# Row maxima of layer 1 turned into rows, value bias folded into the output bias, and a new order of tasks

## The chip, the cores and the metric

One Trainium2 chip, the program on one of its cores. The metric is the device time of one execution in microseconds; of the kernel before, three runs were taken, and the median is the figure that counts.

## The reference, cut to what is computed

The input x is 16 batches of 256 rows by 512, the context 16 x 256 x 384. Four sublayers follow one another, each added to x:

- Layer 0 cross-attention on LayerNorm(x): `Qp = query @ Wq + bq`, K and Q divided by their row norms, 16 heads of 32, softmax of the scaled scores, `out @ Wo + bo`, plus Qp, then LayerNorm with gamma and beta.
- Layer 0 feed-forward: LayerNorm, a Hadamard product, rounding to 4-bit levels by row, a product with ternary weights.
- Layer 1 cross-attention on LayerNorm(x): the parts that matter here are

```
v = (key_value @ Wv + bv) ...
attn = jnp.einsum('bhqd,bhkd->bhqk', q, k) * scale
attn = jnp.clip(attn, -CLAMP, CLAMP)
attn = jax.nn.softmax(attn, axis=-1)
x = jnp.einsum('bhqk,bhkd->bqhd', attn, v).reshape(B, Nq, Cq)
return x @ Wo + bo
```

- Layer 1 feed-forward: LayerNorm, ternary W1 to 2048, GELU, ternary W2 back to 512.

The rows of a softmax sum to one, so `attn @ (kW + bv) @ Wo + bo` equals `attn @ (kW) @ Wo + (bv @ Wo + bo)`.

## The kernel before, in words

**Two phases.** Phase A (about the first 1376 us) does the two attentions and the layer 0 feed-forward, batch by batch. Phase B does the layer 1 feed-forward two batches at a time, and the change doesn't touch it.

**Streams and steps.** A batch passes four streams of tasks: `front_0` (part 0f: norm, turns, projections of q, k and v), `heads_of(0) + back(0)` (0b: scores, exp, attend, output product, feed-forward 0), `front_1` (1f) and `heads_of(1) + back(1)` (1b). In step i, stream n works on batch i-n, so four batches are in work at once. There are 19 steps, 0 to 18. In steps 3 to 15 all four streams are active and the string ORDER merges their task lists: each digit names the stream that gives the next task. ORDERS has an own string for steps 0, 1, 2, 16, 17 and 18, where `PREPARE` adds a fifth stream (weights to split, signs to take). Every engine walks through the same merged list and issues its part of each task, so ORDER sets the order of work on each engine's queue; semaphores make an engine wait where a task's input is not there. The eight PSUM banks are handed out along the same order by `banks_of`.

**Numbers.** Products are made of fp16 halves: `product` (L1285 on) does three matmuls of 512 columns per chunk (L1289, L1290, L1293), and with a bias a fourth one, L1292, of a bias row pair held as [128, 512] and a column that chooses the pair's two rows. `project` tasks with j = 2 are the values; with j = 0 and 1 they are q and k of layer 0. `project_turned` (L1299 to L1303) makes q and k of layer 1 turned, 13 + 13 matmuls of 256 columns for j = 0 (4 chunks of three, and the bias), 10 + 10 for j = 1.

**Layer 1's softmax.** In `front_1`, `maxima` makes the 16 heads' scores with the queries as rows (four heads, a quad, at once, each on 32 rows of the array: L1430), and DVE's `reduce` (L1113) takes each row's maximum. After 8 heads DVE's `shifts` (L1118) clips them into `mcut` [128, 2, 16] fp16. One step later, in `heads_of(1)`, `scores` makes the scores of a quad again, now with the keys as rows, in four PSUM banks. DVE's `clip` (L1123) clips each bank in place. PE's `head` then waits for the clip of its own head and subtracts the maxima, which must now lie along the columns: two matmuls of 256 columns per head (L1445), whose stationary side is the column `mcut[:, q, n]` broadcast to 128 and whose moving side is minus the identity. It then attends head n-4: 12 matmuls of 33 or 32 columns (L1463 to L1465). ScalarE's `head` takes exp (L905) and the upper fp16 half (L913), GpSimd's the lower half (L759). After each quad DVE's `attn_out` divides (L1203, L1206).

**The rest that is named later.** `clip` is the DVE's work at L1123; `out` of layer 0 is L1142 plus statistics (L1031, L1033); `post_norm` is L1152, L1154 and statistics; `split_qk` of layer 1 is L1106; `turn_ffn`, `turn_x`, `turn_out` are four fp32 transposes (L1309); `hadamard` is eight matmuls (L1381). GpSimd computes the reciprocal deviations between DVE's statistics and the next use (L726 to L732). The store of x1 (L774) comes once a step, from GpSimd's queue.

**Setup.** All engines but SP begin by waiting until GpSimd has made CONSTS = 18 constants (L701 to L720). SP loads the first context and x at once, then, after the constants, twelve bias rows (L603). `split_bias` turns them into three fp16 pairs on ScalarE and DVE.

Three places of the code carry this, the merge, the wait per head and the order in the queue:

```
def merged(streams, order):
    streams = [list(x) for x in streams]
    out = [streams[int(n)].pop(0) for n in order]
...
                    pe.wait_ge(clipped.sem, clipped.at(b, n + 1))
...
                        mm = te.matmul(out[:, :, q, :], mcut[:, q, n:n + 1].to_broadcast([P, P]),
                                       minus.unsqueeze(1).to_broadcast([P, NT, P]), start=False, stop=True,
```

Of the kernel before, what the change touches and what calls it, by code (L numbers as in the profile page):

```python
# [63 lines left out]
class Chain:  # L64
# [5 lines left out]
    def __call__(self, ins):  # L70
# [7 lines left out]
ORDER = ("0021312111112210000002010100001110011011100131330003333101033333031133113113102113331133312322102323"  # L78
         "13032123232321321313113031113033131012230120123303230222023222223232121320222020010121220011212")
ORDERS = {  # L80
    0: ("000400000000000440000000000000404000000000000000"),
    1: ("0111111110111040001001101001001011010101010000110111010111011404141414441000100100110000111001011111"
         "01111111404"),
    2: ("2011111121101210011001210012101112000010100101020001011011101012102211020121211200220020000221221111"
         "222220222212220121102012012121021212112101221"),
    B: ("1311333133113113211131112121311211321233413133323333231333321312111214333314313113133411222233121213"
         "3131431222214113123231221322323132221232442222242212121121211"),
    B + 1: ("2334332333333343323322343324333333323423233223343443333224344232233334442222233232322222224223222222"
         "2243223223"),
    B + 2: ("33333333334333433334343333333343333333333343334343344343443444434333"),  # L90
# [10 lines left out]
def fills(task):  # L101
# [4 lines left out]
             "tern_sum": "tw", "tern_turn": "tt", "mean_sum": "ms", "turn_signs": "sg"}  # L106
# [14 lines left out]
def frees(task):  # L121
# [4 lines left out]
              "tern_sum": "tw", "tern_turn": "tt", "mean_sum": "ms", "turn_signs": "sg"}  # L126
# [58 lines left out]
def front_1():  # L185
# [30 lines left out]
def back(l):  # L216
# [13 lines left out]
    0: [("weight", 0), ("weight", 1), ("bias_split", 0), ("weight", 2), ("weight", 3)],  # L230
    1: [("tern_signs", 0), ("tern_sum", 0)] + [("tern_turn", c) for c in range(DC)] + [("weight", n) for n in range(4, 8)],
# [7 lines left out]
APART = [FRONT_TURNS[0] + FRONT_TURNS[1], BACK_TURNS[0] + BACK_TURNS[2], BACK_TURNS[1] + BACK_TURNS[2]]  # L239
STREAMS = [front_0(), heads_of(0) + back(0), front_1(), heads_of(1) + back(1)]  # L240
# [15 lines left out]
def kept_apart(tasks):  # L256
# [3 lines left out]
    late = ("normalise", 1) in at and ("round", 0, 0) in at and at["normalise", 1] > at["round", 0, 0]  # L260
    return all(b < c or d < a for a, b, c, d in pairs) and not late
# [32 lines left out]
def steps(emit):  # L294

    base, kept = [[0] * 8] * 2, {}
    for i in range(B + len(ALL) - 1):
        tasks = task_order(i)
        uses, counts = plan([task for _, task in tasks], base)
        kept.update({name: use for name, use in uses.items() if name[0] in ("tw", "tt", "sg")})  # L300
        emit(tasks, i, i % 2, {**kept, **uses})
        base = plus(base, counts)
# [3 lines left out]
def xattn_ffn(nc, t):  # L306
    with ExitStack() as ctx:
# [25 lines left out]
        half_ones = take(1).bitcast(F16)  # L333
        row_names = ["L0_xattn_bq", "L0_xattn_bk", "L0_xattn_ln_gamma", "L0_xattn_ln_beta"]
        rows = {n: take(D) for n in row_names}
        bias_names = ["L0_xattn_bv", "L0_xattn_bo", "L1_xattn_bq", "L1_xattn_bk", "L1_xattn_bv", "L1_xattn_bo"]
        bias_pairs = [take(D // 2).bitcast(F16) for _ in range(len(bias_names) // 2)]
        bias_rows = {n: (bias_pairs[k // 2], half_ones[:, k % 2:k % 2 + 1]) for k, n in enumerate(bias_names)}
# [69 lines left out]
        mcut = tiny(NT * H // 2).bitcast(F16).rearrange("p (t h) -> p t h", t=NT)  # L408
# [5 lines left out]
        one_col = tiny(1)  # L414

# [28 lines left out]
        CONSTS = 18  # L444
# [1113 lines left out]
```

## Time and profile before

| | |
|---|---|
| median of three runs | 1841.64 us (1840.3 to 1843.56) |
| profiled execution, first to last instruction | 1838.4 us |
| PE busy | 1722.9 us, 94%, 18714 matmuls |
| DVE busy | 1209.7 us, 66% |
| ScalarE busy | 1067.7 us, 58% |
| GpSimd busy | 925.6 us, 50% |
| mean granted TensorE clock | 0.978 |
| L1445, the shift | 512 matmuls |
| L1292, bias of values and of the output product | 128 matmuls |

The profiled execution has no separate device time on record; its span is 3.2 us under the median of the runs, and the median contains what lies around the span. In the rows below matmuls overlap (starts lie closer together than one lasts), so what a matmul costs its successors is read from the distance between starts. "L1123 ... x4" is four instructions in a row, with the time from the first's start to the last's end. A bracket at the end of a row is idle time of the engine before it and what ended it.

### The profile page before, as it was taken

The page shows a single profiled execution, that of the slowest core. Times are in us where ns is not written, and L with a number is a line of the kernel's source. Part 1 is how long each engine was busy: PE and PEld are TensorE (multiplying, and loading weights), DVE is VectorE, ACT ScalarE, POOL GpSimd, SP SyncE. Part 2 cuts the span into 40 slices and gives each one's busy share as a digit, 9 for nine tenths or more (in the row PEclk, how much of TensorE's full clock was granted, in tenths as well). Part 3 has the DMA queues.
Part 4 walks back from the last instruction along what each step waited for, and adds up shares of the span by engine and source line. Part 5 has one row for each costly group of instructions (what it writes and reads, how often), then busy time and mean ns, then how long its engine had stood idle before and what let it go on. Part 6 is the DMA issues. An engine that isn't in the chain of part 4 may idle for free. (4 is left out here: it accounts for less than half of the span.)

```text
span 1838.4 us, 45922 instructions
## 1 busy us (share of the span) xinstructions
PE 1722.9 (94%) x18714; PEld 1052.9 (57%) x18714; DVE 1209.7 (66%) x2446; ACT 1067.7 (58%) x1970; POOL 925.6 (50%) x1062
## 2 busy tenths in 40 slices
PE   5789999999999999999999999979769999999999
PEld 2455666666666666666666666655544444444443
DVE  5658778687786867768687786849973433344332
ACT  5675866868677586876868667576552222222221
POOL 1663846748466484755848467464462222222221
PEclk9789999999999999999999999989979999999999
DMA  7122020211202112020220202045320111011100
GB/s 234 44 86 80 6 96 2 96 51 47 96 2 97 42 56 96 3 96 21 77 92 6 96 2 97 17 158 189 106 97 0 47 47 46 1 46 47 46 24 23
DMA packets 46343, 115.56 MB, mean 63 GB/s; under 512 B 5420, under 2 KB 9644, under 8 KB 45112
## 3 DMA queue, kind: packets, MB, share of 16 engines
q1 hardware_dynamic: 43832, 104.25, 16.4%
q0 software_dynamic: 2304, 8.39, 1.1%
q8 instruction: 150, 2.46, 0.6%
q14 instruction: 57, 0.47, 0.1%
HBM read 72.78 MB, written 31.46 MB: 57 GB/s over the span
## 5 line engine op out<-in xcount | busy, mean ns | idle before, releaser
L759 POOL TENSOR_TENSOR arena<-arena 128x512 f16<-128x512 f32 x512 | 568.8, 1135 | 159.2 <-ACT arena L913 159.1
L905 ACT ACTIVATE arena<-psum 128x512 f32<-128x512 f32 x512 | 309.8, 612 | 54.4 <-PE psum L1430 31.3
L913 ACT ACTIVATE arena<-arena 128x512 f16<-128x512 f32 x512 | 329.2, 651 | 1.0 <-PE psum L1465 1.0
L963 ACT ACTIVATE arena<-psum,arena 128x512 f32<-128x512 f32 x128 | 88.3, 690 | 352.6 <-PE psum L1483 352.6
L1289 PE MATMUL psum<-arena 128*128 128x512 f16 x672 | 258.2, 384 | 7.5 <-ACT arena L905 4.0
L1290 PE MATMUL psum<-arena 128*128 128x512 f16 x672 | 255.4, 380 | 0.0
L1293 PE MATMUL psum<-arena 128*128 128x512 f16 x672 | 255.0, 379 | 0.0
L789 POOL TENSOR_TENSOR arena<-arena 128x512 f16<-128x512 f32 x64 | 73.1, 1142 | 341.4 <-DVE arena L1233 341.4
L1483 PE MATMUL psum<-arena 128*128 128x512 f16 x1024 | 243.6, 380 | 1.4 <-DVE arena L1226 1.4
L1493 PE MATMUL psum<-arena 128*128 128x512 f16 x1016 | 239.9, 378 | 1.0 <-POOL arena L789 1.0
L1233 DVE CAST arena<-arena 128x512 f16<-128x512 f32 x128 | 54.8, 428 | 271.8 <-ACT arena L963 271.8
L1463 PE MATMUL psum<-arena 128*128 128x33 f16 x2048 | 202.0, 179 | 23.1 <-POOL arena L759 21.4
L771 POOL TENSOR_TENSOR arena<-arena 128x512 f32<-128x512 f32 x32 | 41.8, 1329 | 327.3 <-DVE arena L1177 327.3
L1463 PEld LDWEIGHTS psum<-arena 128*128 128x128 f16 x2048 | 171.8, 97 | 54.6 <-issue 18.4
L1465 PE MATMUL psum<-arena 128*128 128x33 f16 x2048 | 199.4, 178 | 0.4 <-issue 0.4
L1464 PE MATMUL psum<-arena 128*128 128x32 f16 x2048 | 199.2, 177 | 0.0
L1309 PE MATMUL psum<-arena 128*128 128x128 f32 x992 | 149.9, 288 | 38.4 <-ACT arena L835 13.5
L1123 DVE TENSOR_SCALAR psum<-psum 128x512 f32<-128x512 f32 x256 | 160.7, 691 | 24.4 <-PE psum L1430 24.2
L1464 PEld LDWEIGHTS psum<-arena 128*128 128x128 f16 x2048 | 166.0, 97 | 13.8
L1042 DVE TENSOR_TENSOR arena<-psum,arena 128x512 f16<-128x512 f32 (+1 forms) x192 | 123.1, 663 | 75.2 <-ACT arena L840 73.9
L1483 PEld LDWEIGHTS psum<-arena 128*128 128x128 f16 x1024 | 99.8, 98 | 124.7 <-issue 2.7
L1430 PE MATMUL psum<-arena 32*128 32x256 f16 x4608 | 163.2, 272 | 8.5 <-DVE arena L1086 3.0
(123 smaller groups left out, 3329.5 us busy)
## 6 DMA issues: line engine op xcount, KB each, us to landing
arena<-in_x SPq DMA_DIRECT2D x32, 512.0 KB, 4.6
arena<-x_scratch SPq DMA_DIRECT2D x32, 512.0 KB, 5.7
arena<-in_L_ffn_W SPq DMA_DIRECT2D x16, 1024.0 KB, 5.2
arena<-arena SPq DMA_DIRECT2D x16, 512.0 KB, 6.5
x_scratch<-arena POOLq DMA_DIRECT2D x16, 512.0 KB, 6.2
x_scratch<-arena SPq DMA_DIRECT2D x16, 512.0 KB, 3.0
out<-arena SPq DMA_DIRECT2D x14, 512.0 KB, 3.8
arena<-in_ctx SPq DMA_DIRECT2D x16, 384.0 KB, 5.7
```

What stands on the lines that cost most here:

```text
L759: gp.tensor_tensor(pl[l][:, h % NP, :], pf[l][:, h % NF, :], ph[l][:, h % NP, :], ALU.subtract).then_inc(p_lo[l].sem, 1)
L905: sc.activation(pf[l][:, h % NF, :], bank(u.bank), ACT.Exp, scale=SCALE / (QS * QS) if l == 0 else SCALE).then_inc(read[u.bank], 1)
L913: sc.activation(ph[l][:, h % NP, :], pf[l][:, h % NF, :], ACT.Copy).then_inc(p_hi[l].sem, 1)
L1289: te.matmul(out, x_hi, w[:, 0, c, :], start=(c == 0), stop=False)
L1290: te.matmul(out, x_hi, w[:, 1, c, :], start=False, stop=False)
L1293: mm = te.matmul(out, x_lo, w[:, 0, c, :], start=False, stop=(c == chunks - 1))
L1430: mm = te.matmul(bank(u.bank)[:, k * S:(k + 1) * S], parts[own][rows_g, j, m, k * P:(k + 1) * P], parts[other][rows_g, 1 - j, m, :], start ...
L1463: te.matmul(out, p_hi_t, vs[l][:, k, h, 0:OW], start=(k == 0), stop=False)
L1464: te.matmul(out[:, 0:HD], p_hi_t, vs[l][:, k, h, HD + 2:VP], start=False, stop=False)
L1465: mm = te.matmul(out, p_lo_t, vs[l][:, k, h, 0:OW], start=False, stop=(k == NT - 1))
L1483: mm = te.matmul(bank(4 + f % 2), w1T[:, c, f * P:(f + 1) * P], xTb[slot][:, part, c, :], start=(c + part == 0), stop=(c + part == DC))
L1493: mm = te.matmul(bank(k), src[:, f % NG, k * P:(k + 1) * P], w2T[:, f, :], start=(f + n == 0), stop=(f + n == FC))
```

## The change

- **Shift by rows.** New task `turn_max` in `front_1`, after each `shifts`: PE multiplies `mcut[:, q, :]` (now [128, 2, 128] fp16, of which the columns 32g + m hold head 4m + g) with minus the identity, two matmuls of 128 columns, which gives the negated maxima as rows; ScalarE copies them as fp16 into `max_turned` [128, 256], one per 8 heads. New task `shift` in `heads_of(1)`, after the four clips of a quad: PE waits for the quad's fourth clip and does four matmuls, one per head and bank, with 32 rows and 512 columns: stationary a column that chooses one of the 32 rows, broadcast to 128, moving `max_turned` repeated twice. `head` no longer shifts.
- **Value bias folded.** The values are projected without bias. Once per layer a new task `fold` computes bv @ Wo in 12 matmuls of 512 columns and adds it to bo in the stage of bias rows; the output product still has its bias matmul, of one tile per layer. GpSimd places bv in columns (`place_bv`); SP loads bv as columns and 8 bias rows instead of 12.
- **Setup.** CONSTS goes from 18 to 21: two memsets of 128x1024 fp16 and one of 128x256 fp16 come in, one memset of 128x512 fp32 goes, and four small additions (three of them in a chain) take the place of three small memsets.
- **Order.** ORDER and all ORDERS are new, and `BEFORE` demands that the last shift of a batch comes before `shifts` and `turn_max` of the next one.

The diff, cut to its core:

```diff
+ORDER = ("2011120111212102000011010000100111013011010333301100300310123113133311302331301133222233103313330331"
+         "3311132223121333132133213331131103011303033112221233003322202203222122322323222202222202001020111201"
+         "1")
...
     for m in range(H // HG):
         out += [("maxima", 1, m)] + [("reduce", 1, h) for h in quad(m)]
         if m * HG % EARLY_MAXIMA == EARLY_MAXIMA - HG:
-            out += [("shifts", 1, m * HG // EARLY_MAXIMA)]
+            out += [("shifts", 1, m * HG // EARLY_MAXIMA), ("turn_max", 1, m * HG // EARLY_MAXIMA)]
...
-            out += [("clip", 1, h) for h in quad(m)]
+            out += [("clip", 1, h) for h in quad(m)] + [("shift", 1, m)]
...
-    0: [("weight", 0), ("weight", 1), ("bias_split", 0), ("weight", 2), ("weight", 3)],
-    1: [("tern_signs", 0), ("tern_sum", 0)] + [("tern_turn", c) for c in range(DC)] + [("weight", n) for n in range(4, 8)],
+    0: [("weight", n) for n in range(4)] + [("fold", 0)],
+    1: [("tern_signs", 0), ("tern_sum", 0)] + [("tern_turn", c) for c in range(DC)] + [("weight", n) for n in range(4, 8)] + [("fold", 1)],
...
-                        mm = product(bank(u.bank), src, wsplit[l, "qkv"[j]], k, n, 2 * late, n if late else 2,
-                                     bias_rows[f"L{l}_xattn_bv"] if j == 2 else None)
+                        mm = product(bank(u.bank), src, wsplit[l, "qkv"[j]], k, n, 2 * late, n if late else 2)
...
+                    elif kind == "turn_max":
+                        u = use["mt", 1, k]
+                        pe.wait_ge(shift_ready.sem, shift_ready.at(b, k + 1))
+                        open_bank(u)
+                        for q in range(NT):
+                            mm = te.matmul(bank(u.bank)[:, q * P:(q + 1) * P], mcut[:, q, :], minus, start=True, stop=True)
+                        mm.then_inc(filled[u.bank], 1)
+                    elif kind == "shift":
+                        if k % 2 == 0:
+                            all_read(pe, [use["mt_before", 1, k // 2]])
+                        pe.wait_ge(clipped.sem, clipped.at(b, HG * k + HG))
+                        for g, h in enumerate(quad(k)):
+                            rows_g = slice(g * HD, (g + 1) * HD)
+                            te.matmul(bank(use["s", 1, h].bank), chosen[rows_g, k:k + 1].to_broadcast([HD, P]),
+                                      max_turned[k // 2][rows_g, :].unsqueeze(1).to_broadcast([HD, NT, S]), start=False, stop=True,
+                                      skip_group_check=True).then_inc(shifted.sem, 1)
...
+                    elif kind == "fold":
+                        u = use["fd", l]
+                        pe.wait_ge(w_split, split_by(l, "o"))
+                        pe.wait_ge(bv_placed, 4 * l + 4)
+                        open_bank(u)
+                        for c in range(DC):
+                            for n, (x, w) in enumerate(((0, 0), (0, 1), (1, 0))):
+                                mm = te.matmul(bank(u.bank), bv_sel[l][:, x, c, :], wsplit[l, "o"][:, w, c, :],
+                                               start=(c + n == 0), stop=(c == DC - 1 and n == 2))
...
-            def head(l, i, b, n, use):
-                if l == 1 and n < H:
-                    if n % EARLY_MAXIMA == 0:
-                        pe.wait_ge(shift_ready.sem, shift_ready.at(b, n // EARLY_MAXIMA + 1))
-                    pe.wait_ge(clipped.sem, clipped.at(b, n + 1))
-                    u = use["s", 1, n]
-                    out = bank(u.bank).rearrange("p (k t n) -> p k t n", k=NT, t=NT)
-                    for q in range(NT):
-                        mm = te.matmul(out[:, :, q, :], mcut[:, q, n:n + 1].to_broadcast([P, P]),
-                                       minus.unsqueeze(1).to_broadcast([P, NT, P]), start=False, stop=True,
-                                       skip_group_check=True)
-                    mm.then_inc(shifted.sem, 1)
+            def head(l, b, n, use):
```

Merged with the streams, the orders give these lists of tasks in a steady step between the scores of quad 2 of layer 1 and the shift of quad 3 (a number after the kind is the layer, the next the tile, head or quad). Before:

```
scores 1 2; clip 1 8; out_project 0 0; out_project 0 1; clip 1 9; clip 1 10; clip 1 11; out 0 0; normalise 1;
head 1 8; turn_x 1 0; turn_x 1 1; out 0 1; norm 0 1; split_x 1 0; head 1 9; split_x 1 1; head 1 10;
post_norm 0 0; head 1 11; unit 0 1; scores 1 3; project_turned 1 0 0; post_norm 0 1; split_qk 1 0 0;
clip 1 12; project_turned 1 0 1; clip 1 13; split_qk 1 0 1; clip 1 14; project 1 0 2 0; normalise_ffn 0 0;
clip 1 15; project 1 0 2 1; normalise_ffn 0 1; head 1 12; turn_ffn 0 0; head 1 13; turn_ffn 0 1;
split_ffn 0 0; head 1 14; turn_qk 0 0 0; head 1 15
```

After:

```
scores 1 2; out_project 0 1; clip 1 8; clip 1 9; clip 1 10; unit 0 1; clip 1 11; shift 1 2; out 0 0;
head 1 8; head 1 9; out 0 1; post_norm 0 0; post_norm 0 1; head 1 10; project_turned 1 0 0; split_qk 1 0 0;
project_turned 1 0 1; head 1 11; normalise_ffn 0 0; split_qk 1 0 1; normalise_ffn 0 1; scores 1 3;
clip 1 12; clip 1 13; turn_ffn 0 0; clip 1 14; project 1 0 2 0; turn_ffn 0 1; clip 1 15; shift 1 3
```

Head 8 carries on DVE the division of the first quad (`attn_out`) in both.

## Rows read from the trace of the kernel before

**Rows 1.** The first line of the page.

```profile
span 1838.4 us, 45922 instructions
```

**Rows 2.** Steady stretch, busy us (instructions): PE, PEld, DVE, ACT, POOL; granted clock, DMA.

```profile
250.00:1150.00 900.00, 878.13 (x11840) 587.18 (x11839) 686.35 (x1466) 662.07 (x1281) 564.24 (x676) 1.00 0.17 58
```

**Rows 3.** GpSimd in order of time (start us, us), the store of x1.

```profile
254.48 0.61 POOL L774 DMA_DIRECT2D x_scratch<-arena  x1 [0.30 <-POOL arena L771]
...
1114.04 0.61 POOL L774 DMA_DIRECT2D x_scratch<-arena  x1 [0.30 <-POOL arena L771]
```

**Rows 4.** PE in order of time: two heads' shift, one head's attend.

```profile
741.95 0.60 PE L1445 MATMUL psum<-arena 128*128 128x256 f16 x4
742.38 0.18 PE L1463 MATMUL psum<-arena 128*128 128x33 f16 x1
...
742.69 0.38 PE L1289 MATMUL psum<-arena 128*128 128x512 f16 x1
```

**Rows 5.** PE in order of time: a bias matmul, a quad of scores.

```profile
707.70 0.38 PE L1292 MATMUL psum<-arena 128*128 128x512 f16 x1
707.92 0.38 PE L1293 MATMUL psum<-arena 128*128 128x512 f16 x1
708.23 0.83 PE L1430 MATMUL psum<-arena 32*128 32x256 f16 x24
709.00 0.39 PE L1289 MATMUL psum<-arena 128*128 128x512 f16 x1
```

**Rows 6.** All engines in order of time, setup.

```profile
4.63 1.54 PE L1309 MATMUL psum<-arena 128*128 128x128 f32 x6 [4.63 <-POOL arena L720]
...
5.43 0.70 DVE L1031 BATCH_NORM_STATS2 arena<-arena 128x6 f32<-128x512 f32 x1 [5.43 <-DMA arena<-in_x]
```

**Rows 7.** DVE in order of time, one steady step.

```profile
521.25 0.69 DVE L1142 SCALAR_TENSOR_TENSOR arena<-psum,arena 128x512 f32<-128x512 f32 x1
...
522.85 0.18 DVE L1203 RECIPROCAL arena<-psum 128x8 f32<-128x8 f32 x1
...
524.00 0.69 DVE L1142 SCALAR_TENSOR_TENSOR arena<-psum,arena 128x512 f32<-128x512 f32 x1 [0.45 <-PE psum L1293]
...
527.06 0.74 DVE L1152 SCALAR_TENSOR_TENSOR arena<-arena 128x512 f32<-128x512 f32 x1
...
529.49 1.64 DVE L1152 SCALAR_TENSOR_TENSOR arena<-arena 128x512 f32<-128x512 f32 x1
...
532.82 0.66 DVE L1106 SCALAR_TENSOR_TENSOR arena<-psum,arena 128x512 f16<-128x512 f32 x1
533.40 1.29 DVE L1123 TENSOR_SCALAR psum<-psum 128x512 f32<-128x512 f32 x2
534.59 0.68 DVE L1106 SCALAR_TENSOR_TENSOR arena<-psum,arena 128x512 f16<-128x512 f32 x1
535.19 1.29 DVE L1123 TENSOR_SCALAR psum<-psum 128x512 f32<-128x512 f32 x2
```

**Rows 8.** PE in order of time, the same step.

```profile
527.83 0.28 PE L1299 MATMUL psum<-arena 128*128 128x256 f16 x1
...
533.52 0.38 PE L1289 MATMUL psum<-arena 128*128 128x512 f16 x1
...
536.20 0.64 PE L1309 MATMUL psum<-arena 128*128 128x128 f32 x4
536.67 0.38 PE L1445 MATMUL psum<-arena 128*128 128x256 f16 x2
```

**Rows 9.** GpSimd in order of time, the same step.

```profile
528.32 2.26 POOL L759 TENSOR_TENSOR arena<-arena 128x512 f16<-128x512 f32 x2
```

**Rows 10.** PE in order of time, step 16.

```profile
1275.94 0.38 PE L1445 MATMUL psum<-arena 128*128 128x256 f16 x2 [1.28 <-DVE psum L1123]
```

**Rows 11.** PE around that wait: stretch, its length, busy us, granted clock, DMA.

```profile
1274.60:1277.80 3.20, 1.38 (x9) 1.00 1.04 397
1277.90:1281.30 3.40, 3.40 (x36) 0.50 0.34 139
```

More of the change, by code:

```diff
@@ L239 @@
 APART = [FRONT_TURNS[0] + FRONT_TURNS[1], BACK_TURNS[0] + BACK_TURNS[2], BACK_TURNS[1] + BACK_TURNS[2]]
+BEFORE = [(("normalise", 1), ("round", 0, 0)), (("shift", 1, H // HG - 1), ("shifts", 1, 0)),
+          (("shift", 1, H // HG - 1), ("turn_max", 1, 0))]
 STREAMS = [front_0(), heads_of(0) + back(0), front_1(), heads_of(1) + back(1)]
@@ L259, in kept_apart, with kept_uses @@
     pairs = [[at[task] for task in x] for x in APART if all(task in at for task in x)]
-    late = ("normalise", 1) in at and ("round", 0, 0) in at and at["normalise", 1] > at["round", 0, 0]
-    return all(b < c or d < a for a, b, c, d in pairs) and not late
+    in_order = all(at[a] < at[b] for a, b in BEFORE if a in at and b in at)
+    return all(b < c or d < a for a, b, c, d in pairs) and in_order
+def kept_uses(uses):
+    kept = {name: use for name, use in uses.items() if name[0] in ("tw", "tt", "sg")}
+    return {**kept, **{("mt_before", *name[1:]): use for name, use in uses.items() if name[0] == "mt"}}
 assert all(kept_apart([task for _, task in task_order(i)]) for i in range(B + len(ALL) - 1))
@@ L299, in steps @@
         uses, counts = plan([task for _, task in tasks], base)
-        kept.update({name: use for name, use in uses.items() if name[0] in ("tw", "tt", "sg")})
         emit(tasks, i, i % 2, {**kept, **uses})
+        kept.update(kept_uses(uses))
         base = plus(base, counts)
@@ L716, in _, with place_bv @@
                 gp.memset(vs[l][:, :, :, HD:HD + 2], 1.0).then_inc(const_ready, 1)
-            gp.memset(half_ones, 0.0).then_inc(const_ready, 1)
-            for n in range(2):
-                pool.wait_ge(const_ready, CONSTS - 2 + n)
-                gp.memset(half_ones[n * 2 * HD:(n + 1) * 2 * HD, n:n + 1], 1.0).then_inc(const_ready, 1)
-            pool.wait_ge(const_ready, CONSTS)
+            for l in range(2):
+                gp.memset(bv_sel[l], 0.0).then_inc(const_ready, 1)
+            gp.memset(mcut, 0.0).then_inc(const_ready, 1)
+            gp.tensor_tensor(row_of, identh[:, 0:4], identh[:, HD:HD + 4], ALU.add).then_inc(const_ready, 1)
+            for n in range(1, P // HD):
+                source = identh[:, 0:HG] if n == 1 else chosen
+                gp.tensor_tensor(chosen, source, identh[:, n * HD:n * HD + HG], ALU.add).then_inc(const_ready, 1)
+                pool.wait_ge(const_ready, CONSTS - (P // HD - 1) + n)
+            def place_bv(l):
+                pool.wait_ge(bv_loaded, 16 * 2)
+                hi, lo = ([bv_sel[l][:, s, :, row:row + 1] for row in (0, HD)] for s in range(2))
+                bv = bv_cols[:, l, :].unsqueeze(2)
+                for place in hi:
+                    gp.tensor_copy(place, bv).then_inc(bv_placed, 1)
+                pool.wait_ge(bv_placed, 4 * l + 2)
+                for place, upper in zip(lo, hi):
+                    gp.tensor_tensor(place, bv, upper, ALU.subtract).then_inc(bv_placed, 1)
             def rstd(name, ts):
@@ L933, in step @@
                         split_weight(l)
-                    elif kind == "bias_split":
-                        split_bias()
+                    elif kind == "fold":
+                        upper_bias(l, use["fd", l])
+                    elif kind == "turn_max":
+                        u = use["mt", 1, at[0]]
+                        act.wait_ge(filled[u.bank], u.filled_at)
+                        sc.activation(max_turned[at[0]], bank(u.bank)[:, 0:S], ACT.Copy).then_inc(read[u.bank], 1)
                     elif kind == "tern_sum":
@@ L1180, in step @@
                         split_weight(l)
-                    elif kind == "bias_split":
-                        split_bias()
+                    elif kind == "fold":
+                        fold_bias(l, use["fd", l])
                     elif kind == "tern_signs":
```

96 lines of the change are left out of this document (55 added, 41 removed).

## The prediction

> **What bounds it now.** The span is 1838.4 us [rows 1], the median of the runs 1841.64, so I add 3.2 us to any span. I read the busy times over a long stretch first, then step marks, then PE and DVE in order of time inside one step. Between 250 and 1150 us PE is busy 878 of 900 us at full clock; DVE 686, ACT 662, POOL 564 [rows 2]. The store of x1 comes once a step, at 254.48 and, 11 steps later, at 1114.04 [rows 3]: 78.1 us a step, of which PE is idle 1.9. PE is the bound, so matmul time taken out counts in full, as long as PE finds its next input ready. ORDER rules the 13 steps in which all four streams run (3 to 15).
>
> **PE time removed.** (a) The shift. Four matmuls of 256 columns (L1445) start the next work 0.43 us later [rows 4], so 0.1075 each; 32 a step are 3.44 us. The new one does four 32-row matmuls of 512 columns per quad. No row shows that form; the nearest is the quad of scores (L1430), 24 matmuls of 256 columns on 32 rows in 0.77 us, which is 0.128 per round of four, and it starts 0.09 us after the slot of the product before it ends (707.92+0.217=708.14, against 708.23) [rows 5]. Two such rounds and the gap give 0.36 a quad, 1.44 a step, which I take, since its row groups and banks are the same. Bounds: 0.22 (one 512-column slot) and 0.87 (no overlap of the four). Gain 2.0 a step, between 2.6 and 0.
> The Trainium skill, "TensorEngine Tiling (Array Packing)", Key Properties, says that a change of tiling mode drains TensorE, which speaks against a new switch per quad. By the row that drain is the 0.09 just counted; the page gives no figure.
> (b) The bias matmul of the values (L1292), 0.217 from its start to the next [rows 5], four a step: 0.87. (c) Added: four matmuls of 128 columns a step (turn_max); by half and by the whole of a 256-column slot 0.2 to 0.43, I take 0.3. Their ACT copy is one of 128x256 twice a step; ACT is idle over a quarter of the stretch [rows 2] and nobody reads the copy before the next step, so nothing; with ACT full it would be about an exp's time each.
> Net 2.57 us a step. Over the 16 batches 41 us. Against it, once: two folds of 12 matmuls (24 x 0.217 = 5.2, partly in idle time of the first steps, 0 to 5.2, I take 4) and longer setup. PE's first matmul starts when GpSimd's constants are done, 4.63; DVE's statistics wait for x until 5.43 [rows 6], so 0.8 is hidden. Three bigger memsets and a chain of four small additions replace one memset and three tiny ones: between 0 and 3 us more, I take 1.8, and 1 shows. SP has 8 small bias row loads instead of 12 plus two loads of columns, before first use in both cases: nothing. The second rounding of weights is as before. If all else stood, 1841.6-41+5 = 1805.
>
> **The wait that the new order adds.** Before, head n of layer 1 waited for its own clip; now the shift waits for the fourth clip of the quad. I expanded both orders and added rows along the two queues, between the scores of quad 2 and the use of quad 3, since DVE can't begin the clips of quad 2 before PE has made those scores.
> DVE, new order: 4 clips, out, attn_out, out, post_norm twice, split_qk twice, 4 clips. From [rows 7]: two clips take 1.19 (533.40 to 534.59), so 2.4 for four; out 1.60 (521.25 to 522.85); attn_out 0.70 (522.85 to 524.00 less the 0.45 waited); the first post_norm 2.43 (527.06 to 529.49), the second 3.33 (529.49 to 532.82); split_qk 0.58. Sum 2.4+1.6+0.7+1.6+2.43+3.33+1.16+2.4 = 15.6, with 0.1 of tail and 0.1 to start: 15.8 us after the scores' slot.
> PE, new order, from the same point to the shift of quad 3: out_project 13 x 0.217 = 2.82, shift 0.36, four heads' attend at 0.31 (742.38 to 742.69) [rows 4] = 1.24, two project_turned 5.69 (527.83 to 533.52), scores 0.86, two turn_ffn at 0.47 (536.20 to 536.67) [rows 8] = 0.94, six matmuls of the values 1.30. Sum 13.2.
> So PE waits 15.8-13.2 = 2.6 us there in each of 13 steps. In the order before, the quad's clips end at 535.19+1.29 = 536.48 [rows 7], and PE makes the second of its four shifts at 536.67 [rows 8], with a feed-forward turn in between and the last two later: no wait. The new order has moved the shift ahead of hadamard and two heads and packed both post_norms before the clips. The same sum for quads 0 and 2 gives slack of 1 and 0.3, for quad 1 a shortage of 0.3. Behind the waiting shift stand attend, hadamard and the next projections on PE; exp waits with it, but POOL's queue has room.
> The second L1152 lasts 1.64 us, the first 0.74 [rows 7]; POOL's pair of subtractions runs from 528.32 to 530.58 [rows 9], and 530.58+0.6 is its end. The Trainium skill, "SBUF — State Buffer", section "SBUF: two separate sides", has GpSimd and a DVE op with two SBUF inputs hold a common port pair exclusively; the trace agrees with it. I keep one collision a step. With none the wait is 1.7, with two 3.5.
>
> **Sum of the likeliest case.** A steady step: -2.57 +2.6, and about 0.5 of today's 1.9 us of small idle spots goes, as DVE is ahead after the wait: -0.5 a step, -6.5 over 13. Steps 16 to 18 save 7.7 and have the same waits for whole quads (three sums like the above come out 2 to 4 us short, against about 1 before): I take 0 net, -6 to +8. Setup and fold +5. Total -1.5, forecast 1841 rounded: no change, its own range 1828 to 1852.
>
> **Rivals.**
> Slower, by the clock. At 1275.94 PE had waited 1.28 us for clips [rows 10]; over 1274.6 to 1277.8 it was busy 1.38 of 3.2 us, and in the next 3.4 us the granted clock was 0.50, the 1.2 GHz level, with PE busy throughout [rows 11]. Such a fall costs 1.7 us. In the steady stretch the clock now never falls [rows 2]. If the new wait at quad 3 makes it fall, at 1.7 times 13: +22, 1863; in half the steps 1852. For: one wait of 2.6 is longer than that one. Against: turn_ffn comes late too, so the wait is probably split in three with a product between them, busy about 60%. It decides from where PE is idle as much as in the row. Chance 0.28.
> The Trainium skill, "TensorE: Matmul & The Clock Gate", "HAM oscillation — how this bites in real kernels", says that gaps which recur each loop can throttle each loop; what this case shows is the row above.
> Faster, the gain kept. The wait is 1 us or less (DVE's pieces shorter in their new places, no collision, clips overlapped better than the rows say), all small idle goes: 1805 to 1828, centre 1815. For: this order's other DVE sums are met within 0.5 us. Against: 15.8 is added from rows of whole sequences. Chance 0.32.
> The 32-row shift isn't concurrent: 0.87 a quad, so (a) gains nothing and the step saves 0.57; the one shift inside the sum above takes 0.5 off the wait. A step is then -0.57+2.1-0.5 = +1.0, and the whole +13+4+5: about 1860. Against: L1430 is the same form. In the slower case's tail, 0.05.
> The likeliest case has the remaining 0.35.
>
> **Chances and range.** 0.2% (about what a measurement tells from no change) is 3.7 us. Faster: 0.31 of the faster case and 0.08 of the likeliest; same 0.18, nearly all the likeliest; slower: 0.33 of the rivals and 0.10. That is 0.39, 0.18, 0.43. The range leaves out the lower third of the faster case and the upper third of the slower: 1807 to 1862.
>
> **What would show it.** The x1 stores 77 to 79 us apart; PE's busy time 40 us less; an idle time of 1.5 to 3 us a step before the shift's matmuls or the turn_ffn just before them, released by the clip. It is wrong if the step is 75 to 76 us with no such wait (the faster case), or if the granted clock in steady steps is below 1.00 (the clock case). L1292 should count 64, and the shift's quad should take about 0.36.

## The result, and the profile after

The changed kernel takes 1870.42 us (median of 4 runs, 1869.37 to 1871.96), against 1841.2 for the kernel before on the same chip: a ratio of 1.0157, 95% interval 1.0143 to 1.0172. It is slower by 29 us, beyond the upper end of the predicted range, 1862. The profiled execution has a span of 1867.6 us against 1838.4 [rows 1].

First the page of the kernel after: span and busy times.

```profile
span 1867.6 us, 45556 instructions
...
PE 1704.5 (91%) x18482; PEld 1014.6 (54%) x18482; DVE 1197.9 (64%) x2444; ACT 1081.2 (58%) x2001; POOL 929.5 (50%) x1073
```

The groups of PE by line, with busy us, mean ns, and idle time before them with what ended it, first after, then the shift before:

```profile
L1413 PE MATMUL psum<-arena 32*128 32x512 f16 x256 | 26.2, 398 | 30.2 <-DVE psum L1164 30.2
L1425 PE MATMUL psum<-arena 128*128 128x512 f16 x24 | 5.5, 379 | 0.1
```
```profile
L1445 PE MATMUL psum<-arena 128*128 128x256 f16 x512 | 95.5, 277 | 11.1 <-DVE psum L1123 9.9 <-POOL arena L759 0.5
```

The work did what the diff says: the old shift counted 512 matmuls, the new one (L1413) 256; the bias matmul of `product` (L1333; L1292 before) counts 64, those of the output product. What is new is the idle time: PE stands 30.2 us in front of the new shift, for the clip (L1164), where it stood 11.1 us in front of the old one.

The steady stretch answers to [rows 2], and below it is one step in which the clock stays up. The stores of x1 answer to [rows 3]:

```profile
250.00:1150.00 900.00, 847.69 (x11339) 547.12 (x11336) 666.75 (x1432) 653.32 (x1264) 548.96 (x653) 0.98 0.18 59
337.32:416.63 79.31, 74.13 (x1013) 47.91 (x1016) 59.52 (x128) 57.94 (x113) 48.74 (x59) 1.00 0.17 57
```
```profile
257.92 0.61 POOL L805 DMA_DIRECT2D x_scratch<-arena  x1 [0.30 <-POOL arena L802]
...
416.63 0.61 POOL L805 DMA_DIRECT2D x_scratch<-arena  x1 [0.30 <-POOL arena L802]
...
496.33 0.61 POOL L805 DMA_DIRECT2D x_scratch<-arena  x1 [0.30 <-POOL arena L802]
...
575.64 0.61 POOL L805 DMA_DIRECT2D x_scratch<-arena  x1 [0.30 <-POOL arena L802]
...
656.87 0.61 POOL L805 DMA_DIRECT2D x_scratch<-arena  x1 [0.30 <-POOL arena L802]
...
1138.28 0.61 POOL L805 DMA_DIRECT2D x_scratch<-arena  x1 [0.30 <-POOL arena L802]
```

(1138.28-257.92)/11 = 80.0 us a step, against 78.1. The single intervals are of three kinds: most are 79.3 (496.33 to 575.64), one is 79.7 (416.63 to 496.33), four are 81.1 to 81.2 (575.64 to 656.87 is the first). PE is idle 52.3 us of this stretch (900-847.7), against 21.9 before; in a clean step, one of 79.3 without a fall of the clock, it is busy 74.1 and idle 5.2, where a step before had 76.2 and 1.9 on average. What PE waited for there (us in total, times, longest), first after, then before:

```profile
PE psum L1517 <- POOL arena L790: 23.6, 47, 0.6
PE psum L1350 <- ACT arena L867: 18.6, 11, 1.7
PE psum L1413 <- DVE psum L1164: 7.3, 6, 1.2
PE psum L1350 <- DVE arena L1247: 2.4, 11, 0.3
```
```profile
PE psum L1309 <- DVE arena L1206: 7.0, 12, 0.6
...
PE psum L1463 <- POOL arena L759: 1.6, 5, 0.3
```

Three places stand out: the attends wait for GpSimd's lower halves (L790, L759 before), 2.1 us a step; the first of the two turn_ffn before the shift of quad 3 waits for ACT's normalise (L867), 1.7 us; the shift of quad 3 waits for the clips, 1.2 us.

The last two waits belong together. PE in order of time around quad 3, in two steps that follow each other: in the first the clock holds, in the second it falls.

```profile
541.96 0.66 PE L1350 MATMUL psum<-arena 128*128 128x128 f32 x4 [1.69 <-ACT arena L867]
...
545.57 0.40 PE L1413 MATMUL psum<-arena 32*128 32x512 f16 x4 [1.22 <-DVE psum L1164]
...
622.79 0.78 PE L1350 MATMUL psum<-arena 128*128 128x128 f32 x4 [1.69 <-ACT arena L867]
...
626.79 0.40 PE L1413 MATMUL psum<-arena 32*128 32x512 f16 x4
```

In the first, PE stands still for 1.69 and 1.22 us, 2.9 in all, with 2.4 us of work between. In the second the products between start 0.43 us apart instead of 0.22, and the shift that ends the chain has no wait left; from the first turn to the shift it is 3.61 and 4.00 us, so the fall costs 0.4 here. VectorE in order of time in the second step:

```profile
610.14 2.49 DVE L1164 TENSOR_SCALAR psum<-psum 128x512 f32<-128x512 f32 x4 [1.50 <-PE psum L1495]
...
616.68 1.07 DVE L1193 SCALAR_TENSOR_TENSOR arena<-arena 128x512 f32<-128x512 f32 x1
...
619.44 0.72 DVE L1193 SCALAR_TENSOR_TENSOR arena<-arena 128x512 f32<-128x512 f32 x1
...
623.86 2.48 DVE L1164 TENSOR_SCALAR psum<-psum 128x512 f32<-128x512 f32 x4
```

From the start of the clips of quad 2 to the end of those of quad 3 it is 16.2 us (626.34-610.14); the prediction had 15.6.

The clock: the prediction read 1.00 for the steady stretch, here it is 0.98. Short stretches: at quad 3 in the first of those two steps, where it holds (the wait, and what follows it); at the same place of the second, where it falls; and behind the waits of the attends.

```profile
538.97:542.37 3.40, 1.71 (x43) 1.35 (x41) 2.56 (x5) 1.28 (x2) 2.80 (x8) 1.00 0.00 0
542.37:545.77 3.40, 2.18 (x17) 1.16 (x15) 3.35 (x6) 1.91 (x4) 2.25 (x3) 1.00 0.01 2
619.80:623.20 3.40, 1.71 (x43) 1.35 (x41) 2.57 (x5) 1.28 (x2) 2.80 (x8) 1.00 0.00 0
623.20:626.60 3.40, 3.40 (x13) 1.75 (x11) 3.35 (x6) 1.32 (x3) 2.26 (x3) 0.50 0.00 0
582.40:585.80 3.40, 3.40 (x40) 2.44 (x37) 1.12 (x2) 2.75 (x7) 3.01 (x3) 0.52 0.76 270
```

There are nine such falls between 250 and 1150, and none before. The place decides what they cost. Five are at quad 3, on top of the wait for the clips: one of them (462.8) is alone in its step, and that step is the one of 79.7, 0.4 us more than its neighbours, as the 0.4 from turn to shift says. The four like 582.4 stand behind the attends' waits, each in a step that has one at quad 3 too, and those are the four steps of 81.2: 1.9 more, so 1.5 for the fall behind the attends. All falls of the thirteen steady steps together are then 5 x 0.4 + 4 x 1.5 = 8 us.

**Where the 29 us are.** By the marks: the first store of x1 comes 5.6 us later (113.53 against 107.97), the next interval is 2.6 shorter, the thirteen steady ones are 22 longer (1038.9 against 1017.0), the interval behind them 6.2 shorter, and from the last store (1294.07 against 1275.33) to the end it is 10.4 longer.

### The profile page after: what moved, and what is told of

Same layout as the page of the kernel before. It is cut to its first block, busy times and chain, and to the rows that moved or that the text cites. A ratio compares the mean times of both kernels' runs of the same rounds, so it can differ in the third digit from the quotient of the medians.

```text
span 1867.6 us, 45556 instructions
## 1 busy us (share of the span) xinstructions
PE 1704.5 (91%) x18482; PEld 1014.6 (54%) x18482; DVE 1197.9 (64%) x2444; ACT 1081.2 (58%) x2001; POOL 929.5 (50%) x1073
## 4 chain that ended last, share of the span: by engine, by line
PE 60%; DVE 13%; POOL 12%; issue 3%; ACT 2%; DVEq 0%; ACTq 0%
PE psum L1537 12%; PE psum L1547 12%; POOL arena L790 7%; PE psum L1330 6%; PE psum L1334 5%; PE psum L1331 5%; PE psum L1495 5%; PE psum L1350 5%; DVE psum L1164 5%; PE psum L1446 3%; PE psum L1517 2%; POOL arena L802 2%; PE psum L1519 2%; DVE arena L1070 2%; PE psum L1518 2%
## 5 line engine op out<-in xcount | busy, mean ns | idle before, releaser
L790 POOL TENSOR_TENSOR arena<-arena 128x512 f16<-128x512 f32 x512 | 561.1, 1120 | 137.0 <-ACT arena L945 136.2
L822 POOL TENSOR_TENSOR arena<-arena 128x512 f16<-128x512 f32 x64 | 73.2, 1143 | 338.1 <-DVE arena L1274 338.1
L1517 PE MATMUL psum<-arena 128*128 128x33 f16 x2048 | 192.6, 179 | 48.0 <-POOL arena L790 47.6
L1517 PEld LDWEIGHTS psum<-arena 128*128 128x128 f16 x2048 | 165.3, 96 | 89.9 <-POOL arena L790 51.0
L1519 PE MATMUL psum<-arena 128*128 128x33 f16 x2048 | 189.7, 178 | 0.0
L1518 PE MATMUL psum<-arena 128*128 128x32 f16 x2048 | 189.5, 178 | 0.0
L1164 DVE TENSOR_SCALAR psum<-psum 128x512 f32<-128x512 f32 x256 | 160.6, 692 | 41.3 <-PE psum L1495 41.1
L1518 PEld LDWEIGHTS psum<-arena 128*128 128x128 f16 x2048 | 163.7, 97 | 11.4
L1537 PEld LDWEIGHTS psum<-arena 128*128 128x128 f16 x1024 | 99.7, 97 | 125.7 <-issue 3.8
L1081 DVE TENSOR_TENSOR arena<-psum,arena 128x512 f16<-128x512 f32 (+1 forms) x192 | 121.7, 662 | 70.5 <-ACT arena L872 70.5
```

The source lines that it names most:

```text
L790: gp.tensor_tensor(pl[l][:, h % NP, :], pf[l][:, h % NF, :], ph[l][:, h % NP, :], ALU.subtract).then_inc(p_lo[l].sem, 1)
L1164: v.tensor_scalar(bank(u.bank), bank(u.bank), CLAMP / SCALE, -CLAMP / SCALE, ALU.min, ALU.max).then_inc(clipped.sem, 1)
L1517: te.matmul(out, p_hi_t, vs[l][:, k, h, 0:OW], start=(k == 0), stop=False)
L1518: te.matmul(out[:, 0:HD], p_hi_t, vs[l][:, k, h, HD + 2:VP], start=False, stop=False)
L1537: mm = te.matmul(bank(4 + f % 2), w1T[:, c, f * P:(f + 1) * P], xTb[slot][:, part, c, :], start=(c + part == 0), stop=(c + part == DC))
```

## The experiments

Ten kernels ran. A "steady step" is the interval of the x1 stores that most steps show; each was compared with the kernel before on its own chip (single runs 1837.6 to 1845.9 us, medians 1839.8 to 1841.0). Steps, waits and falls are those of the one profiled execution.

**The order and the arithmetic apart.** The first kernel has the new arithmetic with the order before (turn_max, shift and fold put where their inputs come):

```
-ORDER = ("2011120111212102000011010000100111013011010333301100300310123113...
+ORDER = ("0021312111112210000002010100001110011011100131330003333310103333...
```

> The changed arithmetic in the order of before: ORDER and ORDERS of before, with each shift put just before the first head of its quad, each turn_max just before the next maxima, the folds at the end of steps 0 and 1. If the new order is what costs (my theory), the gain of 2.57 us a step stays, less what the wait for the quad's fourth clip costs there: 1803 to 1820 us, x1 stores 75 to 76.5 us apart, clock 1.00 in steady steps. If the new arithmetic itself costs (a shift that waits for four clips, in any order), 1850 us or more, with waits before the shift of over 3 us a step.

> The kernel before, with its own arithmetic, in the new order (shift, turn_max and fold left out of the lists). If the new order is what costs, this is slower than before by what it added in waits and falls of the clock: 1855 to 1890 us. If the arithmetic is what costs, it stays within 5 us of 1841.

Measured: 1925.8 us, ratio 1.0468 (1.0452 to 1.0483) for the new arithmetic in the old order, steady step 81.4 to 82.5; 1910.4 us, 1.0386 (1.0368 to 1.0404) for the old arithmetic in the new order, steady step 82.7. Both are worse than either kernel. The first meets the case against my theory in its time (1850 or more), the second is beyond the 1855 to 1890 of the case for it. So "the order costs it" is as wrong as "the arithmetic costs it": each arithmetic does better in its own order. PE's waits between 250 and 1150, first of the new arithmetic in the old order, then of the old in the new:

```profile
PE psum L1405 <- DVE arena L1158: 26.9, 22, 2.1
PE psum L1413 <- DVE psum L1164: 17.4, 22, 1.0
...
PE psum L1517 <- POOL arena L790: 4.1, 11, 0.4
```
```profile
PE psum L1463 <- POOL arena L759: 14.8, 33, 0.6
```

The new arithmetic brings two waits of its own, each twice a step: turn_max waits for VectorE's shifts (L1158), the row shift for the fourth clip. The new order hides the first wholly (2.7 us in the whole kernel after) and the second in part. GpSimd's lower halves go with the order and not with the arithmetic: one wait a step in the order of before (4.1 us), three or four in the new one (14.8, and 23.6 in the changed kernel).

**The bias fold alone.** The shift as before and the order before, only the value bias folded into the output bias.

```
-                        mm = product(bank(u.bank), src, wsplit[l, "qkv"[j]], k, n, 2 * late, n if late else 2,
-                                     bias_rows[f"L{l}_xattn_bv"] if j == 2 else None)
+                        mm = product(bank(u.bank), src, wsplit[l, "qkv"[j]], k, n, 2 * late, n if late else 2)
```

> Only the value bias folded, in the order of before, with the old shift of two matmuls per head. Both theories: 64 matmuls of 512 columns less at 0.217 us, 13.9 us, and 24 more once, 5.2, and about 1 us of longer setup: 1832 to 1836 us. Under 1829 would mean that the folds are hidden in idle time, over 1839 that taking out PE work in a steady step gains nothing.

Measured: 1837.91 us, 0.9989 (0.998 to 0.9998); most steady steps 77.2 to 77.3, 0.8 to 0.9 less than 78.1, as predicted. The thirteen steps together are 10.4 us shorter, but the kernel only 2, and the expectation (1832 to 1836) is missed. The rest is in one interval, that behind the first store: 77.1 us against 67.7. The fold of layer 1 stands in it:

```profile
111.83 4.66 PE L1421 MATMUL psum<-arena 128*128 128x512 f16 x12 [7.05 <-POOL arena L750]
```

L1421 is the fold. PE stands 7.0 us before it until GpSimd has placed the bias, and the 12 matmuls then last 4.7 us, at a granted clock of 0.50, instead of 12 x 0.217 = 2.6. The prediction's 4 us for both folds counted their matmuls and not whom they wait for. In the changed kernel the fold (L1425) waits 0.1 us: its order has put it later.

**The clock.** Six matmuls with no use (the next product overwrites them) in the first product of the project task of V, between the two waits at quad 3:

```
+                        if (l, k, j, late) == (1, 0, 2, 0):
+                            for c in range(6):
+                                te.matmul(bank(u.bank), src[:, 0, c % 2, 0:P], wsplit[1, "v"][:, 0, c % 2, :], start=True, stop=True)
```

> The changed kernel with six extra matmuls of 512 columns (1.3 us at full clock) in layer 1's first value projection, between the two waits of quad 3, their result overwritten. If PE waits there anyway and the falls of the clock are half of the loss, the falls in steady steps go and the time drops to 1848 to 1860 us. If the falls come from somewhere else, nothing or less than 5 us is gained, 1866 to 1872. If PE doesn't wait there, 16 times 1.3 come on top: 1885 to 1892.

Measured: 1873.16 us, 1.0184 (1.0167 to 1.0201). The time lies between two of the expected cases and meets neither. The six matmuls, 1.3 us, cost nothing in the undisturbed steps (79.3), which shows the room at quad 3. The falls between 250 and 1150 went from nine to four: those behind the attends from four to one, those at quad 3 from five to three. But the extra matmuls have used up the room, and a fall at quad 3 alone now makes a step of 81.0, 1.7 more and not 0.4; the step with both falls took 82.4. The thirteen steady steps are 1039.1 us together, the changed kernel's 1038.9: fewer falls, and the same price for them in sum.

**VectorE's chain.** The mean's subtraction and gamma of layer 0's post_norm (L1193, twice a step) left out:

```
-                        chain(v.scalar_tensor_tensor(out=res0[:, k, :], in0=res0[:, k, :], scalar=mv["E"][:, k, 0:1],
-                                                     in1=rows["L0_xattn_ln_gamma"], op0=ALU.subtract, op1=ALU.mult))
```

**GpSimd's queue.** The lower halves of the first four heads of layer 0 computed for half their columns, from the second batch on:

```
+                            n = S if l == 0 and h < HG and b > 0 else NT * S
-                            gp.tensor_tensor(pl[l][:, h % NP, :], pf[l][:, h % NF, :], ph[l][:, h % NP, :],
+                            gp.tensor_tensor(pl[l][:, h % NP, 0:n], pf[l][:, h % NF, 0:n], ph[l][:, h % NP, 0:n],
```

> The changed kernel without the multiplication by gamma and the mean's subtraction (L1193) in post_norm, so two DVE operations a step leave the chain between the scores of quad 2 and the shift of quad 3. If the wait at quad 3 is DVE's queue, it shrinks by their 1.8 us, the step goes from 80.0 to 78 or less and the time to 1838 to 1850. If that wait has another cause (the banks, ScalarE, the array's change of mode), under 5 us are gained.

> The changed kernel with GpSimd's lower halves of heads 0 to 3 of layer 0 over half of the columns, so GpSimd has about 2.1 us less to do at the step's start. If attend waits there for GpSimd's queue, the waits of 1.5 us before the first four attends go, and the step is 1 to 1.8 us shorter: 1845 to 1857. If they stand behind PE's other waits anyway, 1865 to 1872.

> Both cuts at once. If the two waits are separate, the gains add, and with less idle time the clock stays up in steady steps: a step of 76 to 77.3 us and 1815 to 1832 us. If the step is set by something else, it is near the better of the two alone.

Measured:

| kernel | median us | ratio (95%) | steady step | falls, 250 to 1150 |
|---|---|---|---|---|
| changed | 1870.42 | 1.0157 (1.0143 to 1.0172) | 79.3 / 81.2 | 9 |
| post_norm shorter | 1845.73 | 1.0022 (1.0009 to 1.0035) | 78.0 | 1 |
| lower halves shorter | 1857.54 | 1.0091 (1.0076 to 1.0106) | 79.1 | 1 |
| both | 1837.04 | 0.9981 (0.9971 to 0.9991) | 77.8 | 0 |

PE's waits, 250 to 1150: post_norm shorter, then lower halves shorter (its code has one line more, so L791 is the lower half):

```profile
PE psum L1515 <- POOL arena L790: 24.1, 48, 0.6
PE psum L1411 <- DVE psum L1164: 13.4, 11, 1.2
PE psum L1348 <- ACT arena L867: 4.2, 11, 0.4
```
```profile
PE psum L1496 <- ACT arena L938: 13.8, 24, 0.9
...
PE psum L1518 <- POOL arena L791: 7.0, 12, 0.6
```

With a shorter post_norm the wait for the normalise goes from 18.6 to 4.2 us: that is VectorE's chain, by way of ACT. The step falls by 1.3, and the time lies in the expected 1838 to 1850. Its profiled execution took 1840.96 us at a granted clock of 0.974, and seven of its ten runs took 1845 to 1846.5 at 0.969 to 0.970, so the clock was down for longer in them, and the step and the one fall of the table are those of a fast execution. That fall (963.5) is behind the attends and alone in its step: 79.5 us against 78.0, the 1.5 found above. With shorter lower halves GpSimd's wait goes from 23.6 to 7.0, but scores (L1496) now wait 13.8 us for exp (L938) and the step falls only by 0.2, where 1 to 1.8 was expected: GpSimd's wait hid another that comes behind it. Yet the time falls by 12.9 us. The thirteen steady steps give 9.9 of it: 13 x 0.2 are 2.5, and 7.4 came with the falls, of which one is left (at quad 3, in a step of 79.6 against 79.1). So the clock's part of the 29 us is about 8 in the steady steps. Both cuts together missed their 1815 to 1832: the gains do not add, as the wait for exp stays at 13.8 us and the shift's at 13.4.

**One task moved.** The project task of V behind the shift of quad 3 put ahead of it:

```
-         "3311132223121333132133213331131103011303033112221233003322202203222122322323222202222202001020111201"
+         "3311132223121333132132313331131103011303033112221233003322202203222122322323222202222202001020111201"
```

> The changed kernel with one task moved in ORDER: the last three matmuls of layer 1's first value projection (0.65 us) come before the shift of quad 3, not after it. If PE only waits there for DVE's clips, the 0.65 us fill the wait, 8 us less over 13 steps, 1860 to 1864, fewer falls of the clock may add to it. If the wait is set by PE's own queue, no difference.

Measured: 1863.78 us, 1.0128 (1.0106 to 1.0149); steady step 78.9, 81.3 in those with a costly fall. The longest wait at L1413 is 0.6 us instead of 1.2, as the 0.65 us of product that was moved under it says, and the time is in the expected 1860 to 1864. The step gains 0.4 of it, since some 0.2 comes back as a new wait of the attends (L1517 for VectorE's L1081: 1.3 us in 7 waits). GpSimd's and the normalise's waits are untouched (23.5 and 18.5 us). There are nine falls between 250 and 1150 as before, but five of the thirteen steps are long, not four: this profiled execution took 1868.29, the slowest of four, and its thirteen steps are only 1.1 us shorter than the changed kernel's. The two fastest runs took 1861.9 and 1862.0 at a granted clock of 0.968 against 0.964. Between executions of this one kernel the time moves by 6 us, and the clock with it, as much as the moved task gains.

**The order fitted again.** The last two have every instruction of the changed kernel and another string for steps 3 to 15.

```
-ORDER = ("2011120111212102000011010000100111013011010333301100300310123113...
+ORDER = ("0211101112212100201000000310011101001110113003110330031310302131...
```

> The arithmetic of the changed kernel, every instruction as it is, with another string of tasks for the steps in between (3 to 15); the first and last steps as in the changed kernel. The project task of V and the second turn_ffn stand elsewhere beside the shift of quad 3, and the order of clips, transposes and heads around it is another. Theory A (the 3.4 us wait at the clips, 2.0 at GpSimd's lower halves and 1.7 at the normalise are matters of placement, and the work saved, 2.6 us a step, is real): steady step 76 to 77 us, no fall of the clock in the steady steps, 1825 to 1838. Theory B (VectorE's chain of a step is the bound, wherever the tasks stand): steady step 78 or more and the wait for the clips stays near 3 us, 1845 to 1865.

> As the run before, with a third string for the steps in between, which differs from it in some forty places (the project task of V stands behind the shift of quad 3 as in the changed kernel). Theory A: 1822 to 1838, steady step 76 to 77 us. Theory B: 1845 to 1865, steady step 78 or more. If the two strings differ by more than 5 us, placement alone moves the time by as much as the whole arithmetic does.

Measured: 1829.27 us, 0.9931 (0.9917 to 0.9945), and 1829.16 us, 0.9935 (0.9923 to 0.9948). Both beat both kernels, as theory A expected. The steady stretch of the first, and the longest and the shortest of PE's waits in it:

```profile
250.00:1150.00 900.00, 863.72 (x11802) 558.85 (x11800) 698.20 (x1487) 678.21 (x1321) 569.94 (x691) 1.00 0.18 58
```
```profile
PE psum L1350 <- DVE arena L1145: 16.0, 24, 0.8
...
PE psum L1517 <- POOL arena L790: 0.3, 1, 0.3
```

Its x1 stores at 254.99 and 1102.53 make (1102.53-254.99)/11 = 77.0 us a step (most intervals 76.8). The waits for clips are gone and those for GpSimd nearly (in the second string they are 7.8 and 0.7 us), and no fall is left in the stretch. So VectorE's chain isn't the bound of a step (theory B), the string was. Of the 29 us the string of steps 3 to 15 holds all and more: 41. Each string differs from the changed kernel's in many places at once, so what each place gives is not known. A new fit of the string for the old arithmetic was not tried, so that the 12 us under the kernel before come from the arithmetic alone is not shown either.

**What it does not mend.** These kernels keep the changed kernel's last steps, and from the last store of x1 to the end they take 572.8 and 574.6 us, the changed kernel 573.5, the kernel before 563.1 (1838.4-1275.33). The stretch of 130 us that begins 5 us before the last store, after, then before; and what PE waited for in it, after:

```profile
1289.00:1419.00 130.00, 86.60 (x1091) 57.44 (x1091) 94.62 (x140) 63.29 (x105) 65.07 (x47) 0.79 0.31 104
```
```profile
1270.00:1400.00 130.00, 101.90 (x1173) 64.94 (x1172) 102.39 (x151) 64.03 (x106) 66.94 (x48) 0.89 0.31 106
```
```profile
PE psum L1413 <- DVE psum L1164: 14.7, 7, 2.7
```

Where layer 1's heads have few products beside them, the shift waits up to 2.7 us for its whole quad, seven times; before, each head waited for its own clip (L1445, nine waits, 6.8 us in all, 1.7 the longest). GpSimd's waits are 11.9 against 6.1 us. And the clock is lower, 0.79 against 0.89: between 1360 and 1390 it was granted at 0.50 throughout, while PE was busy half of the time, and in the same place before (1341.3 to 1371.3) it was 0.83. How the 10 us divide among these, and how much is the order of those steps, was not tried by itself. From the last store to the end the old arithmetic in the new order takes 569.4 us and the new one in the order of before 580.7.

## Why the prediction was wrong

It said 1841, no change (its own sum gives 1840, and that of the rival without concurrency 1864, not 1860); the likeliest case's wait came, with two other things on top. By its steps:

- **PE time removed: right in kind, 0.5 a step too large.** L1333 counts 64, and the fold alone gave 0.8 to 0.9 a step. But a clean step has 74.1 us of PE work, 2.1 less than the 76.2 before, not 2.57. A shift of a quad that follows a product:

```profile
357.65 0.38 PE L1334 MATMUL psum<-arena 128*128 128x512 f16 x1
357.96 0.40 PE L1413 MATMUL psum<-arena 32*128 32x512 f16 x4
358.29 0.19 PE L1517 MATMUL psum<-arena 128*128 128x33 f16 x1
```

  It takes 0.33 us to the next start, and the product in front keeps its place for 0.31 instead of 0.217: 0.42 for the quad, where 0.36 with this gap inside was taken. Two matmuls of turn_max take 0.2, so 0.4 a step where 0.3 was taken. That is 0.35 of the 0.5; the rest has no row. The four row matmuls do overlap (without it, 4 x 0.217 = 0.87), so the rival "not concurrent" is out. The Trainium skill, "TensorEngine Tiling (Array Packing)", Key Properties, says that a change of tiling mode drains TensorE; the 0.09 in front agrees with it. PE's busy time fell by 18 us in all and not by 40: besides the 0.5 a step, the mean clock is 0.966 instead of 0.978, and matmuls at the lower level last longer.
- **The wait at quad 3: right in place, somewhat small.** VectorE 16.2 where 15.6 was summed. PE's idle time is 1.69 and 1.22 us, 2.9 for the predicted 2.6, split over a turn_ffn and the shift as the prediction thought possible. One post_norm subtraction took 1.07 and the other 0.72, so of the collision counted (1.64 against 0.74) about 0.35 was there; in the step before this one it was 0.7 (1.42 and 0.72), and the same 16.2 in all. The chain was longer all the same, with waits in it, 0.74 for ACT in both steps.
- **"POOL's queue has room" failed.** This is the step that put the forecast out: waits were summed at the quads of layer 1 alone, and GpSimd was put at nothing by its share (564 of 900 us), with no row of where PE reads from it. GpSimd and PE in order of time where a step's first four attends of layer 0 stand, after, then before:

```profile
577.79 4.23 POOL L790 TENSOR_TENSOR arena<-arena 128x512 f16<-128x512 f32 x4
```
```profile
579.02 0.18 PE L1517 MATMUL psum<-arena 128*128 128x33 f16 x1 [0.32 <-POOL arena L790]
...
581.03 0.19 PE L1517 MATMUL psum<-arena 128*128 128x33 f16 x1 [0.56 <-POOL arena L790]
...
582.08 0.19 PE L1517 MATMUL psum<-arena 128*128 128x33 f16 x1 [0.58 <-POOL arena L790]
```
```profile
569.34 4.23 POOL L759 TENSOR_TENSOR arena<-arena 128x512 f16<-128x512 f32 x4
```
```profile
570.58 0.18 PE L1463 MATMUL psum<-arena 128*128 128x33 f16 x1 [0.33 <-POOL arena L759]
...
572.01 0.18 PE L1463 MATMUL psum<-arena 128*128 128x33 f16 x1
...
575.52 0.18 PE L1463 MATMUL psum<-arena 128*128 128x33 f16 x1
```

  GpSimd's queue is the same in both: the x1 store, the small rstd operations, then four lower halves in a row, 4.23 us, begun 2.1 us after the store (567.20 before, 575.64 after). The string changed what PE does meanwhile. Before, ten transposes, four transposes and nine product matmuls stood between these attends; after, six transposes behind the first and nothing behind the second and third, so PE goes at GpSimd's pace of 1.05 us a head. This is some 2.1 us a step, and the sum had zero. A step with the clock up is then -2.1 of work, +2.1 here, +2.9 at quad 3, +0.2 for the turn behind L1247, and -1.9 for the small waits of before, all of which went (only 0.5 had been counted as going): +1.2, which is what was measured (79.3 against 78.1), where -0.5 was forecast. The fitted strings show that another placement takes GpSimd's wait away; shorter lower halves alone gave 0.2, as the wait for exp stood behind.
- **The clock: named as a rival, and a part of it came.** The prediction made it an alternative to its own case at 0.28; it was an addition to it. It looked for falls at quad 3 and priced them at 1.7; the wait that they stand on hides all but 0.4. The costly ones, 1.5 each, stand behind the GpSimd waits that it had missed, in 4 of 13 steps. The Trainium skill, "TensorE: Matmul & The Clock Gate", section "HAM oscillation — how this bites in real kernels", describes a loop in which a recurring gap throttled every pass; here the waits recur in each step, but a costly fall came in none of the first five steps and in every second one from the sixth to the twelfth.
- **Steps 16 to 18, "0 net, -6 to +8": 4 us too low.** The interval behind the steady ones gained 6.2 and the tail lost 10.4, so +4, inside the bounds. Setup and fold: the first store is 5.6 late and 2.6 of it come back: 3 where 5 was taken.
- **The range** took the two troubles as rivals, each against a faster case, and never both. The thirteen steady steps were forecast at -6.5 and came at +21.9: 8 of the difference are falls, 20.5 are waits and work. 1840 with these two, 2 less at the start and 4 more at the end is 1870.
- **The faster rival** (1805 to 1828) did not come. With this arithmetic and two fitted strings 1829 was reached, 1 us above it; no run came lower.

## What to carry over

When a change comes with a new hand-written order, sum the queue of every engine at every place where PE reads from it, not only at the place that the change is about. A share of 63% says nothing about four operations in a row: the same four made PE wait 1.6 us in 900 with work between the reads, and 23.6 without. Do this as well for whom a new task waits (the fold: 7 us for GpSimd, before 2.6 us of matmuls). And before an arithmetic that saves time on the bound engine is given up, fit the order to it: the same work took 1925.8, 1870.4 and 1829.2 us in three orders.

## What the runs showed of the hardware

- A fall of PE's clock costs what the work in it is short of slack. At quad 3, on a wait of 1.2 us, it cost 0.4 us (steps of 79.7 and 79.3); behind the attends 1.5 (79.5 and 78.0 with the shorter post_norm); at quad 3 with the wait filled by six matmuls 1.7 (81.0 and 79.3).
- The same wait did not always give the same clock. In the two steps shown, PE was busy 1.71 of 3.4 us at quad 3 in both (538.97 and 619.80), and in the next 3.4 us the clock was 1.00 in one and 0.50 in the other. With the shorter post_norm GpSimd's waits are 24.1 us in the stretch, as large as in the changed kernel (23.6), and there was one fall. What tells them apart stays open.
- Four matmuls of 512 columns on four groups of 32 rows took 0.33 us to the next start and 0.09 before them, against 0.22 for one on 128 rows: they overlap, at about twice the slot of one.
- One VectorE operation with two inputs from SBUF (128x512 f32) took 0.72 us, and 1.07 and 1.42 us while GpSimd's lower halves ran (615.07 to 617.21 and 534.24 to 536.38).
